# Counting edges by one-hot rows: the destinations' rows are made on GpSimd instead of VectorE

## What is computed

```python
edge_index = jnp.stack([src, dst])
h = jnp.maximum(_layernorm(x), 0.0)
x = x + _L0_gnn_ref(h, edge_index, ...)      # 4 blocks: conditioned norm, attention over edges, MLP
h = jnp.maximum(_layernorm(x), 0.0)
x = x + _L1_gnn_ref(h, edge_index, ...)      # 2 convolutions: segment_sum(norm * h[src], dst)

# attention in a block
scores = einsum('ehd,ehd->eh', q[src], k[dst])
attn = softmax of scores over the edges of one src
out  = segment_sum(attn * v[dst], src)
```

## Time and profile before

| | |
|---|---|
| median of 3 runs | 1974.06 us (lowest 1970.08) |
| the profiled execution | 1968.63 us, span 1966.9 us |
| TensorE busy | 1889.4 us (96%) |
| VectorE busy | 1365.6 us (69%) |
| ScalarE busy | 781.9 us (40%) |
| GpSimd busy | 449.5 us (23%) |

### The profile page before, as it was taken

How to read it: one execution, slowest core, us unless ns; L and a number is a source line. 1 busy time by engine, 2 the same in 40 slices (tenths; PEclk the granted TensorE clock), 3 DMA queues, 4 the chain that set the end, 5 groups by cost and what they waited for, 6 DMA issues and landing times. The chain is left out here.

```text
span 1966.9 us, 33580 instructions
## 1 busy us (share of the span) xinstructions
PE 1889.4 (96%) x11664; PEld 1561.2 (79%) x11664; DVE 1365.6 (69%) x2830; ACT 781.9 (40%) x1527; POOL 449.5 (23%) x525
## 2 busy tenths in 40 slices
PE   6989999999999999999999999999999998999999
PEld 3446888998889899988998999889989997765443
DVE  7887568888875588878647888885498887630111
ACT  1332545555432355544224554542254554330000
POOL 1000243111332511114224111251341113500000
PEclk9999999999999999999999999999999999999999
DMA  4123452111200112021102110301121117010001
GB/s 136 39 51 66 132 175 90 37 50 42 92 33 33 47 51 58 25 76 46 43 22 83 37 36 25 121 1 43 49 56 37 36 31 195 6 51 0 0 21 31
DMA packets 50720, 108.36 MB, mean 55 GB/s; under 512 B 18144, under 2 KB 18196, under 8 KB 50609
## 3 DMA queue, kind: packets, MB, share of 16 engines
q1 hardware_dynamic: 50608, 106.87, 18.6%
HBM read 83.60 MB, written 23.25 MB: 54 GB/s over the span
## 5 line engine op out<-in xcount | busy, mean ns | idle before, releaser
L781 ACT ACTIVATE PT<-ps 125x500 fp32r<-125x500 f32 (+1 forms) x480 | 214.2, 520 | 323.8 <-PE ps L1588 323.8
L1495 PE MATMUL ps<-PT,V 125*128 125x250 f32 x2400 | 313.2, 284 | 1.6 <-DVE PT L1166 1.6
L1495 PE MATMUL ps<-kT,qg 128*125 128x512 f32 (+1 forms) x1440 | 302.6, 354 | 7.1 <-DVE nmx L1150 5.9
L1495 PEld LDWEIGHTS ps<-PT,V 125*128 125x128 f32 x2400 | 289.6, 190 | 2.9 <-DVE PT L1166 2.9
L1495 PEld LDWEIGHTS ps<-kT,qg 128*125 128x125 f32 x1440 | 245.9, 186 | 57.9 <-issue 10.4
L1166 DVE TENSOR_TENSOR PT<-ps,PT 125x500 fp32r<-125x500 f32 (+1 forms) x480 | 253.1, 582 | 2.0 <-ACT PT L781 1.8
L1150 DVE CUSTOM_DVE_ANT_0 SB<-ps,bt 125x1250 f32<-125x1250 f32 x140 | 204.0, 1457 | 46.9 <-PE ps L1495 44.5
L1588 PE MATMUL ps<-ident,pbuf 125*125 125x125 f32 x1600 | 202.4, 274 | 13.2 <-DVE pbuf L1159 13.2
L1588 PEld LDWEIGHTS ps<-ident,pbuf 125*125 125x125 f32 x1600 | 187.2, 189 | 16.1 <-DVE pbuf L1159 15.4
L775 ACT ACTIVATE pbuf<-SB,nmx 125x1250 f32<-125x1250 f32 x140 | 188.1, 1344 | 8.7 <-DVE nmx L1150 7.0
L1159 DVE TENSOR_SCALAR pbuf<-pbuf,rden 125x1250 f32<-125x1250 f32 x160 | 149.9, 937 | 5.6
(11 more groups left out here) (193 smaller groups left out, 2708.0 us busy)
## 6 DMA issues: line engine op xcount, KB each, us to landing
bt<-edge_bias_scratch SPq DMA_DIRECT2D x40, 546.9 KB
q_scratch<-qc SPq DMA_DIRECT2D x16, 500.0 KB, 2.6
qc<-q_scratch SPq DMA_DIRECT2D x16, 500.0 KB, 4.7
counts_scratch<-cblk SPq DMA_DIRECT2D x10, 546.9 KB
c_rows<-counts_scratch SPq DMA_DIRECT2D x10, 546.9 KB
edge_bias_scratch<-b_rows SPq DMA_DIRECT2D x10, 546.9 KB
counts<-counts_scratch SPq DMA_DIRECT2D x10, 546.9 KB
wm<-in_L_gnn_wo_dram SPq DMA_DIRECT2D x4, 1024.0 KB, 8.3
```

What stands on the lines that cost most here:

```text
L781: sc.activation(PT[:, h % 2, 0, a:b, u * T:(u + 1) * T], ps_T[0:T, i, 0:(b - a) * T].rearrange("p (t n) -> p t n", n=T), ACT.Copy).then_in ...
L1495: e = mm(out_, lhs(a), rhs(b), start=start and i == 0, stop=stop and i == 2)
```

## The change

The comparisons for `oh_dst` leave VectorE's loop and become a loop of GpSimd, `dst_one_hots`, with a semaphore of its own, `onehotd`. For each trio GpSimd copies the three columns of destinations into `dcol` (one instruction of 125 x 3), waits for that copy, and makes three comparisons of 125 x 125, each behind its slot's `oh_used`. The next copy waits for the comparisons before it. TensorE waits for both semaphores. GpSimd splits the norm weights after tile 7 and copies the condition chunk after tile 9; before, both waited for the condition, and nothing of counting stood around them.

```diff
+            def dst_one_hots(t):
+                ring = t % 2
+                first = pool.value_load(tab[0:1, t:t + 1], ...)
+                trios = pool.value_load(tab[0:1, NT + t:NT + t + 1], ...)
+                before = 0 if t < 2 else pool.value_load(tab[0:1, 2 * NT + t:2 * NT + t + 1], ...)
+                with pool.Fori(0, trios) as i:
+                    used = pool.snap((before + i) * TRIO)
+                    chunk0 = pool.snap(...)
+                    pool.wait_ge(s[f"onehotd{ring}"], used + TRIO)
+                    settled(pool)
+                    g.tensor_copy(dcol[:, ring, :], edgeT[:, 1, bass.ds(chunk0, TRIO)]).then_inc(s[f"dcol{ring}"], TRIO)
+                    pool.wait_ge(s[f"dcol{ring}"], used + TRIO)
+                    settled(pool)
+                    for b in range(TRIO):
+                        slot = ring * TRIO + b
+                        pool.wait_ge(s[f"oh_used{ring}"], used + (b + 1))
+                        settled(pool)
+                        g.tensor_scalar(oh_dst[:, slot, 0:T], iota16[:, t * T:(t + 1) * T], dcol[:, ring, b:b + 1], None,
+                                        ALU.is_equal).then_inc(s[f"onehotd{ring}"], 1)
...
+            for t in range(NT):
+                dst_one_hots(t)
+                if t == NT - 3:
+                    split_ln(0)
             pool.wait_ge(s["condS"], 1)
-            split_ln(0)
             cond_chunk(0, PROJECTED[0])
...
                         dve.wait_ge(s[f"oh_used{ring}"], used + (b + 1))
-                        v.tensor_scalar(oh_dst[:, slot, 0:T], iota16[:, t * T:(t + 1) * T],
-                                        edgeT[:, 1, bass.ds(chunk0 + b, 1)], None, ALU.is_equal)
                         v.tensor_scalar(oh_src[:, slot, :], iota16[:, :], edgeT[:, 0, bass.ds(chunk0 + b, 1)], None,
                                         ALU.is_equal).then_inc(s[f"onehot{ring}"], 1)
...
                         slot = ring * TRIO + q
+                        pe.wait_ge(s[f"onehotd{ring}"], done + (TRIO + q + 1))
                         pe.wait_ge(s[f"onehot{ring}"], done + (q + 1))
```

More of the change, by code:

```diff
@@ L191, in build @@
         oh_dst = early("oh_dst", [T, 2 * TRIO, T + 1], BF16)
+        dcol = early("dcol", [T, 2, TRIO])
         iota16 = early("iota16", [T, N], F16)
@@ L241, in build @@
         for name in ("x_ld edge_ld small_ld brow_ld ident consts edge_f edge_t edgeT brow_t cols emb_u emb_r emb_f emb emb_h "
-                     "h1 cond_mm condT rm rel cand cand_t red red_t tab prefix tabi onehot0 onehot1 oh_used0 oh_used1 ct_mm ct ct_t ct_e "
+                     "h1 cond_mm condT rm rel cand cand_t red red_t tab prefix tabi onehot0 onehot1 onehotd0 onehotd1 dcol0 dcol1 oh_used0 oh_used1 ct_mm ct ct_t ct_e "
                      "i_st c_ld0 c_ld1 bln bmask bdone bst_out0 bst_out1 cnt_out0 cnt_out1 condS0 condS lnhi lnS onesr "
@@ L441, in _ @@
                 pool.sem_inc(s[f"oh_used{ring}"], TRIO)
+                pool.sem_inc(s[f"onehotd{ring}"], TRIO)
             g.memset(ident[:, :], 0.0).then_inc(s["ident"], 1)
@@ L478, in _ @@
             pool.wait_ge(s["consts"], CONSTS)
+            def dst_one_hots(t):
+                ring = t % 2
+                first = pool.value_load(tab[0:1, t:t + 1], min_val=0, max_val=ECP - TRIO)
+                trios = pool.value_load(tab[0:1, NT + t:NT + t + 1], min_val=1, max_val=EC // TRIO + 1)
+                before = 0 if t < 2 else pool.value_load(tab[0:1, 2 * NT + t:2 * NT + t + 1], min_val=0, max_val=(EC // TRIO + 1) * NT)
+                with pool.Fori(0, trios) as i:
+                    used = pool.snap((before + i) * TRIO)
+                    chunk0 = pool.snap((first + i * TRIO).with_bounds(min_val=0, max_val=ECP - TRIO))
+                    pool.wait_ge(s[f"onehotd{ring}"], used + TRIO)
[9 more added lines that the diff above has]
+                                        ALU.is_equal).then_inc(s[f"onehotd{ring}"], 1)
             def split_ln(i):
@@ L496, in cond_chunk @@
                 g.tensor_copy(condc[:, :], condS[:, bass.ds(c * W, W)].bitcast(F32)).then_inc(s["condc"], 1)
+            pool.wait_ge(s["tabi"], 1)
+            pool.wait_ge(s["edgeT"], 1)
+            pool.wait_ge(s["prefix"], 3)
+            for t in range(NT):
+                dst_one_hots(t)
+                if t == NT - 3:
+                    split_ln(0)
             pool.wait_ge(s["condS"], 1)
-            split_ln(0)
             cond_chunk(0, PROJECTED[0])
```

## The result

The changed kernel takes 2034.3 us (2030.9 to 2034.6), the kernel before, on the same chip, 1972.1 us (1969.4 at the lowest): ratio 1.032, interval 1.030 to 1.033. It is slower by 62 us, where 25 were forecast. One of the four executions of the kernel before took 10176 us; with it the median is 1972.1, without it 1970.1, and the loss 64 us.

What follows compares the result with a forecast made beforehand. VectorE was taken to bound counting, narrowly, at 0.62 us a chunk. 145 chunks at 0.77 us (+22 us), tile 8's gap (+2) and GpSimd's table loads (+1) made +25 on 1971: 1996 us, range 1964 to 2038.

Steps and rivals of the forecast that it cites:

- trio at a price of 0.29 us: Counting: three chunks on GpSimd, with turns at the port, take 2.31 us, 0.77 us a chunk instead of 0.62.
- whole change at that price: Whole kernel: +25 us on 1971, giving 1996 us.
- chunks that pay the difference: Counting: 145 of 186 chunks run at the slower pace, the others lying ready or in half-clock stretches; +22 us.
- TensorE's clock: Counting: a clock drop was no case of its own; with 2.25 us busy in 4 it kept 1.00.
- norm split between tiles 7 and 8: Tile 8: GpSimd's 2.33 us split widens the gap before it; +2 us of 0 to 2.3.
- the price of the comparison: Counting, GpSimd: a 125-column comparison takes 0.29 us, estimated from casts and a one-input select.
- The end kept for the other side, 0.46: Counting, GpSimd: upper price of a comparison, from the two-input subtract; gives a trio of 2.65 us.
- Turns: Counting: VectorE and GpSimd alternate at a shared port; source comparison holds it 0.41 us, GpSimd's comparison delays VectorE 0.15.
- the prediction's figure by whole durations: Counting: strict turns for whole instructions, 0.54 + 0.29 + 0.19/3, give 0.89 us a chunk.
- The waits around the copy: Counting, GpSimd: 0.28 us ahead of each trio's copy and 0.18 us between copy and first comparison.
- C: Counting: GpSimd comparison of 0.46 us or more, or slow register waits; slower by over 2%, 2010 to 2044; chance 0.30.
- the sign named for it: Counting, GpSimd: a smallest comparison of 0.4 us or more would show the slower-by-over-2% rival.

Runs made afterwards that it cites:

- run 1: Kernel before, with single GpSimd instructions added late, where VectorE does little: a 125-column comparison took 0.60 us, the cast of the same shape 0.289; no kernel time given.
- run 12: Changed kernel with each GpSimd comparison replaced by a cast of 125 columns, waits and copy kept: 1978.0 us, ratio 1.004 to the kernel before.
- run 6: Changed kernel with VectorE's three weight splits moved out of the counting tiles to behind the last tile: 2027.4 us.
- run 10: Changed kernel with one more TensorE matmul of 512 zero columns behind each chunk: 2027.6 us.
- run 7: Changed kernel with GpSimd's split of the norm weights put back behind all tiles: 2034.3 us.
- run 8: Kernel before, with 62 threes of 125-column GpSimd comparisons that nobody reads or waits for, beside counting: 1990.9 us, ratio 1.010.
- run 9: Kernel before, with 62 threes of 125-column GpSimd casts that nobody reads or waits for, beside counting: 1975.6 us, ratio 1.002.
- run 2: Changed kernel whose VectorE source comparison writes only 2 of 1250 columns, the rest zeroed once: 2009.1 us, ratio 1.019 to the kernel before.
- run 4: Changed kernel without the copy of three columns and the two waits around it, comparisons taking a fixed column: 2013.1 us, ratio 1.021 to the kernel before.
- run 5: Changed kernel with GpSimd making only each trio's third destination row, VectorE the other two: 1986.4 us, ratio 1.008 to the kernel before.
- run 3: Changed kernel whose GpSimd destination comparison writes only 2 of 125 columns, the rest zeroed once: 1994.2 us, ratio 1.012 to the kernel before.

## Why the prediction was wrong in size

Its direction and its place were right: GpSimd becomes the bound, counting alone gets longer. The time even lies inside the stated 1964 to 2038, near its end, but the change is two and a half times the forecast. The steps, against what was measured:

| step | prediction | measured |
|---|---|---|
| comparison on GpSimd, alone | 0.29 us (other end 0.46) | 0.60 (run 1) |
| trio at a price of 0.29 us | 2.31 us | 2.16 (run 12) |
| whole change at that price | +25 us | +7.5 us (run 12) |
| trio of the changed kernel | 2.31 us (2.65 at 0.46 us a comparison) | 2.90 us |
| chunks that pay the difference | 145 | 15 of 18 in tile 2 |
| comparisons held by the weight splits | no term | about 8 us of counting (run 6) |
| TensorE's clock | "no case of its own" | at least 7 us (run 10), about 8 us of counting (run 6) |
| norm split between tiles 7 and 8 | +2 us | 1.6 us of counting, nothing in the time (run 7) |

**The step that failed is the price of the comparison.** It was made from casts, since the comparison "has one streamed input", and from a select (0.292 us for 128 columns). The cast and the comparison have the same shape, types and count of inputs, and still differ by 0.31 us. The end kept for the other side, 0.46, was no bound either: it came from the two-input form, which run 1 shows to be cheaper than the comparison. The two kernels that differ in this instruction alone are run 12 and the changed kernel: +7.5 us and +62 us over the kernel before. So 55 us of the 62 hang on it, with the stops and the lost clock that come with it; 186 x 0.31 us are 58.

**Turns exist, and were too large.** The exclusion was read off subtracts of two tensors, which do hold GpSimd (run 6). The one-hot comparison holds it less: a pair of VectorE's and a comparison on GpSimd cost each other 0.18 us (run 8), and a cast costs VectorE some 0.03 (run 9) where the prediction had 0.15 for it. At 0.29 us the sum came out 17 us too high, which hid part of the wrong price. The trio accounts for 7 of them (145 x 0.05); the rest was not measured term by term, but the six fast chunks of a tile (run 12) are part of it. In the changed kernel turns take 0.28 us of the trio (run 2), with VectorE idle for 43% of the time. The Trainium skill, "SBUF — State Buffer", Who interferes with whom, lets the engine that issues first hold the port pair for its whole instruction. For the splits the trace agrees, one comparison standing for 4.66 us beside two of them. For the source comparison, if it runs in a two-port mode, it doesn't: a pair that took 0.62 us and a 0.60 us comparison should then need over 1.1 us (0.54 + 0.60), and needed 0.80. That the prediction's figure by whole durations, 0.89 us a chunk, comes nearer to the measured 0.97 than its own 0.77 is luck: with the price of 0.60 it would be 1.20.

**The waits around the copy** were 0.31 and 0.37 us, together 0.68, where the sum had 0.28 and 0.18. That is 0.22 us a trio, up to 14 us. (The 0.18 was itself a rounding up: 2.7 us over 16 cases are 0.17.) No run isolates what it cost.

**The number of chunks** was about right. Tile 2, without a stop or half clock, went from 14.9 to 20.2 us from closing to closing, and 5.3 / (0.97 - 0.62) is 15 of its 18 chunks: the first trio was ready, as forecast. TensorE began the tile 3.6 us behind the closing of the one before, in both kernels. With the measured pace the prediction's own sum gives 145 x 0.35 + 3 = 54 us of the 65 by which counting ended later. The other 11, net, have no term in it: the holds by VectorE's weight splits, which it did not look for, and the half clock behind them. In run 6, without them, the ninth tile was closed 15.9 us earlier. (The parts don't add up exactly, since tiles 1 and 8, partly at half clock before, lost only 1.8 and 3.5 us.)

**The clock** was dismissed by a row in which TensorE kept 1.00 while it was busy for 2.25 us of 4. That row stands; it was not the kind of stretch that counting got, and a stop as long as the splits brought wasn't in the forecast. Behind TensorE's stop of 2.02 us in tile 3 it was at 0.50 from 100 to 105 us, and up to 210 us the granted clock, read in windows of 5 us, fell at some seven places instead of two.

Among the rivals, C (slower by over 2%, from a comparison of 0.46 us or more, with a chance of 0.30) is the one that came true, inside its 2010 to 2044, and the sign named for it, a smallest comparison of 0.4 us or more, was seen. Its chance was too low: no row showed a comparison on GpSimd, and the time rested on that one number.

**What stays open.** Why the form with one tensor and a scalar costs 2.5 ns a column when the cast costs nothing like it wasn't found. Nor was it settled at which moment of VectorE's comparison GpSimd gets in. Why the clock fell in two single trios (130 to 140 and 155 to 160 us) of the changed kernel, whose like kept full clock in run 6, isn't known. Runs 6 and 10 each gave back 7 us, and they weren't combined.

## What to carry to other kernels

Before work is moved to another engine, run the very instruction there, in its form and size, alone, and take no neighbour's price for it: here a cast and a comparison of the same shape differed by a factor of two, and that was 55 of 62 us. Bounds taken from other forms are no bounds. An engine whose pace sets a loop pays for everything that stands before its instruction (a copy of three columns took 0.9 us with its waits, and leaving it out gave back 21 us), and moving a third of the rows is no way out when each of them comes back to the same slot. And look for the other engine's long instructions that the new work will meet: three subtracts of 2.28 us cost some 16 us of counting, about half as holds and half as lost clock.

## What the runs showed of the hardware

- On GpSimd a comparison or subtract of one tensor with a scalar takes 0.29 us and 2.5 ns a column (0.295, 0.602 and 0.914 us for 2, 125 and 250 columns). A cast of 125 columns takes 0.289 us, a two-input subtract 0.397.
- A VectorE subtract of two float32 tensors (2.28 us) stops GpSimd's comparison nearly for its whole time. In a row of three, one comparison stood through the first two (4.66 us instead of 0.60) and ended beside the third. VectorE's comparisons against a column cost GpSimd's 0.18 us (a pair, run 8), 0.28 (source rows alone, run 4, median) or 0.38 (run 5, median and steady trio).
- From 45 to 175 us, with the same trios (TensorE idle for 1.0 of 2.90 us), the granted clock was 1.00 in run 6, where TensorE's longest stop was 1.30 us, and 0.90 in the changed kernel, where the splits stopped it for 2.02, 2.02 and 2.42 us.
- Work of no use made the kernel faster: 186 matmuls of zeros took 7 us off, as the granted clock rose from 0.90 to 0.96.
- An instruction of two columns on GpSimd (0.295 us alone) was held more beside VectorE's comparisons than a cast of 125 (median 0.56 against 0.29 us, run 3 against run 12). No run shows why.
